# Rope partners by transfers and two packed products in the first attention of a four-layer transformer kernel

## What is computed

```python
xn = layernorm(x)                                  # over the 128 features
q, k, v = (xn @ W + b, split into 2 heads of 64)   # for Wq, Wk, Wv
# features 0..31 of a head are "content", 32..63 are "spatial"
q_spatial, k_spatial = rope(q[..., 32:]), rope(k[..., 32:])
#   rope: x1, x2 = first 16, last 16 of the spatial features
#   [x1 * cos - x2 * sin, x1 * sin + x2 * cos]
attn = softmax(q @ k.T / sqrt(64))                 # 256 x 256 for each sequence and head
x = x + (attn @ v) @ Wo + bo
```

## Time and profile before

| | |
|---|---|
| three executions, us | 712.37, 713.66, 716.26 (median 713.66) |
| the profiled execution, us | 717.27 |
| its span, us | 715.5 |
| busy share of the span: PE / weight loads / DVE / ACT / POOL | 92% / 64% / 70% / 63% / 59% |
| granted TensorE clock, mean | 0.98 of full speed |
| DMA traffic | 52.47 MB |

### The profile page before, as it was taken

One profiled execution on the slowest core, in us unless ns is written; L12 is line 12 of the kernel. 1 busy time (PEld: TensorE's weight loads), 2 busy tenths in 40 slices (PEclk: granted clock), 3 DMA queues, 4 the chain that ended last, 5 costly groups with the idle time before them and its releaser, 6 DMA issues.

```text
span 715.5 us, 14025 instructions
## 1 busy us (share of the span) xinstructions
PE 657.6 (92%) x4713; PEld 457.9 (64%) x4716; DVE 497.8 (70%) x958; ACT 450.6 (63%) x801; POOL 425.5 (59%) x443
## 2 busy tenths in 40 slices
PE   3789998689999999997999999998989999999997
PEld 1455555477777877665555555554546777787785
DVE  6769998665657768556788888885678566775521
ACT  3668887446566666545676677775765556566664
POOL 4544543267777786633345645653666777778673
PEclk9989999899999999999999999998999999999999
DMA  6101230000000000560457666663221000000000
GB/s 195 41 22 42 53 42 2 1 1 1 1 0 0 0 1 2 162 245 7 149 186 235 210 211 225 231 205 137 77 80 47 1 15 16 15 0 15 16 16 29
DMA packets 33028, 52.47 MB, mean 73 GB/s; under 512 B 4560, under 2 KB 9680, under 8 KB 32976
## 3 DMA queue, kind: packets, MB, share of 16 engines
q1 hardware_dynamic: 32784, 51.53, 23.0%
q10 hardware_dynamic: 192, 0.26, 0.1%
HBM read 27.15 MB, written 24.38 MB: 72 GB/s over the span
## 4 chain that ended last, share of the span: by engine, by line
PE 63%; DVE 14%; ACT 8%; issue 7%; DMA 4%; POOL 1%; SPq 1%; DVEq 0%; ACTq 0%; POOLq 0%
PE banks L220 60%; ACT b_prob L1525 4%; DVE xn L182 2%; DVE a_mx L652 2%; ACT a_prob L553 2%; DMA f_h_lo<-b_k_dram 2%; DMA b_o_dram<-b_o 1%; PE banks L212 1%; DVE f_gate L1088 1%; DMA b_k_dram<-b_k_lo 1%; DVE f_h_hi L1091 1%; PE banks L977 1%; DVE f_hidden L1094 1%; DVE a_prob L666 1%; ACT f_g_hi L1044 1%
## 5 line engine op out<-in xcount | busy, mean ns | idle before, releaser
L1158 POOL TENSOR_TENSOR f_g_lo<-f_gelu,f_g_hi 128x512 fp32r<-128x512 f32 x127 | 162.9, 1291 | 54.0 <-ACT f_g_hi L1044 53.4
L1043 ACT ACTIVATE f_gelu<-banks,cols 128x512 f32<-128x512 f32 x128 | 88.3, 690 | 130.6 <-PE banks L220 108.6
L1624 DVE TENSOR_REDUCE b_segment_max<-banks 128x6 f32<-128x768 f32 x128 | 120.2, 950 | 31.1 <-PE banks L220 30.4
L1741 POOL TENSOR_SCALAR_AFFINE_SELECT b_prob<-b_prob 128x512 f32<-128x512 f32 x128 | 81.6, 638 | 93.5 <-ACT b_prob L1525 92.8
L220 PE MATMUL banks<-f_g_hi,whi 128*128 128x512 f32 x320 | 130.2, 407 | 1.9 <-POOL f_g_lo L1158 1.4
L220 PE MATMUL banks<-f_g_lo,whi 128*128 128x512 f32 x320 | 126.7, 396 | 0.0
L1525 ACT ACTIVATE b_prob<-banks 128x768 f32<-128x768 f32 x128 | 102.4, 807 | 38.5 <-PE banks L220 38.2
L1151 POOL TENSOR_TENSOR f_h_lo<-f_hidden,f_h_hi 128x512 fp32r<-128x512 f32 x60 | 77.5, 1292 | 64.5 <-DVE f_hidden L1094 62.8
L220 PE MATMUL banks<-f_h_hi,whi 128*128 128x512 f32 x256 | 104.5, 408 | 5.4 <-POOL f_h_lo L1151 2.7
L220 PE MATMUL banks<-f_h_lo,whi 128*128 128x512 f32 x256 | 101.7, 397 | 0.0
L1044 ACT ACTIVATE f_g_hi<-banks,cols 128x512 fp32r<-128x512 f32 x128 | 87.4, 683 | 0.0
(11 more groups left out here) (125 smaller groups left out, 1093.6 us busy)
## 6 DMA issues: line engine op xcount, KB each, us to landing
f_h_hi<-b_q_dram SPq DMA_DIRECT2D x16, 512.0 KB, 4.0
f_h_lo<-b_k_dram SPq DMA_DIRECT2D x16, 512.0 KB, 5.0
b_o_dram<-b_o SPq DMA_DIRECT2D x8, 1024.0 KB, 4.4
b_q_dram<-b_q_hi SPq DMA_DIRECT2D x16, 256.0 KB, 3.2
b_k_dram<-b_k_hi SPq DMA_DIRECT2D x16, 256.0 KB, 3.0
w_stage<-in_wF SPq DMA_DIRECT2D x8, 352.0 KB, 3.3
b_q_dram<-b_q_lo SPq DMA_DIRECT2D x8, 256.0 KB, 3.6
b_k_dram<-b_k_lo SPq DMA_DIRECT2D x8, 256.0 KB, 3.2
```

Source lines behind the costliest of these rows:

```text
L1043: nc.scalar.activation(gf[c % 2][:, :], z_bank[c % 2], ACT.Gelu, scale=scale).then_inc(s_gf, 1)
L1158: nc.gpsimd.tensor_tensor(lo[:, c, :], gf[c % 2][:, :], hi[:, c, :].bitcast(F32), ALU.subtract).then_inc(s_glo[c % 2], 1)
L1624: nc.vector.reduce_max(seg[:, g, s, 2 * p:2 * p + 2, :], first_pass[:, 2 * p:2 * p + 2, 0:3 * P].rearrange("p b (c k) -> p b c k", c=3), A ...
L1741: nc.gpsimd.affine_select(out=pr, in_=pr, compare_op=ALU.is_ge, fill=0.0, base=0, pattern=[[0, 4], [1, P]], channel_multiplier=-1).then_in ...
```

## The change

- The columns of Wq and Wk are reordered on the host into two matrices of 128 columns: "content" (the 32 content features of q and k of both heads) and "spatial" (the same of the spatial ones). Two products take the place of four. The factor 1/sqrt(64) moves into the q rows.
- ScalarE copies the spatial product out of its bank and adds the bias (`act_raw`). Eight transfers of 16 rows swap the halves of each group of 32 rows (`sp_moves`), VectorE multiplies the copy by the cosines (`dve_spatial`) and the swapped copy by the sines (`dve_swapped`), GpSimd adds them, once a block.
- ScalarE copies the content product (`act_content`). Four transfers of 32 rows bring its parts to `qT` and `kT`, and four more bring the spatial parts. The scores wait for all eight.
- The probabilities are not scaled. The output product is made for each head apart, and VectorE adds it to x with the inverse sum as the factor, tile by tile (`dve_update`, 8 instructions a block).
- The maximum is negated in the reduction. The shift is made on GpSimd. The statistics are taken a block sooner (`b.after(3)`).
- The pieces of weights are issued between the transfers of the blocks.

```diff
@@ sp_program, sp_moves (new)
                 sp.dma_start(X[:, 2 * TILES:, :], x_dram[:, 2 * TILES:, :]).then_inc(s_x2, 16)
+                blocks = [Block(i // 2, i % 2) for i in range(BLOCKS)]
+                for n in blocks:
+                    sp_moves(sp, n)
+                    if n.t >= 1:
+                        for piece in blocks[2:4] if n.t == 1 else blocks[n.t + 2:n.t + 3]:
+                            ffn["sp_piece"](sp, piece, False)
+            PIECES = HA * 2
+            ROWS_A = P // PIECES
+            SWAPS = 2 * PIECES
+            def sp_moves(sp, n):
+                t = n.t
+                half = ROWS_A // 2
+                wait(sp, s_tu, t)
+                sp.wait_ge(s_raw, t + 1)
+                for at in range(0, P, ROWS_A):
+                    for to, of in ((at, at + half), (at + half, at)):
+                        sp.dma_start(swapped[to:to + half, :], raw[of:of + half, :]).then_inc(s_sw, 16)
+                wait(sp, s_sc, SEQS * (t - 1))
+                sp.wait_ge(s_co, t + 1)
+                for g in range(PIECES):
+                    h, to = g // 2, (qT, kT)[g % 2][n.odd]
+                    sp.dma_start(to[DA * h:DA * h + HALF_A, :],
+                                 content[ROWS_A * g:ROWS_A * (g + 1), :]).then_inc(s_mc, 16)
+                sp.wait_ge(s_ro, t + 1)
...
@@ products
+            def pe_T(pe, n):
+                wait(pe, s_vr, n.t)
+                norm.pe(pe, n, misc)
+            def pe_spatial(pe, n):
+                pe.wait_ge(s_xT, n.t + 1)
+                wait(pe, s_raw, n.t)
+                project(spatial_bank, wA[:, W_SPATIAL, :], xnT[n.odd][:, :]).then_inc(s_ws, 1)
...
@@ pe_body
                 pe_scores(pe, b, 1)
                 if one:
-                    pe_proj(pe, n1, "k")
-                for h in (1, 0):
+                    if before:
+                        pe.wait_ge(s_done, b.t - 1)
+                    pe_v(pe, n1)
+                for h in range(HA):
                     pe_probT(pe, b, 0, h)
-                if one:
-                    pe_proj(pe, n1, "kr")
+                if two:
+                    pe_T(pe, n2)
                 pe_pv(pe, b, 0)
-                if one:
-                    pe_proj(pe, n1, "v")
+                if two:
+                    pe_spatial(pe, n2)
...
                     pe_out(pe, b.after(-1))
                 if one:
                     pe_scores(pe, n1, 0)
...
@@ act_body
-                act_normalise(act, b, 0)
                 if before:
                     act_out(act, b.after(-1))
-                for h in (1, 0):
+                if two:
+                    norm.act_apply(act, n2)
+                for h in range(HA):
                     act_probT(act, b, 0, h)
+                if two:
+                    act_xT(act, n2)
                 act_exp(act, b, 1)
                 if two:
-                    norm.act_apply(act, n2)
-                act_normalise(act, b, 1)
-                if two:
-                    act_xT(act, n2)
+                    act_raw(act, n2)
+                    if not is_block(b, 0):
+                        ffn["beside"]["act"](act, n2)
...
                     act_exp(act, n1, 0)
+                if two:
+                    act_content(act, n2)
@@ dve_swapped, dve_update, dve_body
+            def dve_swapped(dve, n):
+                dve.wait_ge(s_sw, 16 * SWAPS * (n.t + 1))
+                wait(dve, s_ro, n.t)
+                nc.vector.tensor_tensor(as_seqs(turned[:, :]), as_seqs(swapped[:, :]),
+                                        S[:, :].unsqueeze(1).to_broadcast([P, SEQS, T]), ALU.mult).then_inc(s_tu, 1)
...
+                for s in range(TILES):
+                    x = X[:, bass.ds(TILES * b.t + s, 1), :]
+                    last = nc.vector.scalar_tensor_tensor(
+                        out=x, in0=tiles_of(bank)[:, s:s + 1, :], scalar=inv[b.odd][:, s // 2, h, s % 2:s % 2 + 1],
+                        in1=x, op0=ALU.mult, op1=ALU.add)
...
                 dve_max(dve, b, 1)
...
+                    dve_v(dve, n1)
+                if three(b):
+                    dve.wait_ge(norm.shift, b.t + 1)
+                    norm.dve_stats(dve, b.after(3))
...
+                    dve_inverse(dve, b.after(-1))
+                    dve_update(dve, b.after(-1), 0, content_bank)
                 if one:
                     dve_max(dve, n1, 0)
...
+                    dve_update(dve, b.after(-1), 1, misc)
+                if two:
+                    dve_spatial(dve, n2)
+                    dve_swapped(dve, n2)
                     ffn["beside"]["dve"](dve, n2)
```

More of the change, by code:

```diff
@@ L339, in attention_a @@
             s_in_ = sem("a_inverse_total")
-            s_no = [sem(f"a_probabilities_normalised{h}") for h in range(HA)]
             s_pt = [sem(f"a_probabilities_transposed{h}") for h in range(HA)]
@@ L531, in pe_last @@
                 nxt["pe_gate"](pe, FIRST_BLOCK, 1, parts)
-                for h in (0, 1):
+                for h in range(HA):
                     pe_probT(pe, LAST_BLOCK, 1, h)
@@ L663, in dve_normalise @@
[L663 to L673 removed]
+                wait(dve, s_ex, UNITS * (b.t - 1) + HA * (s + 1))
@@ L675, in dve_body, with three @@
+            def three(b):
+                return not (isinstance(b.t, int) and b.t > BLOCKS - 4)
             def dve_body(dve, b, before, one, two):
```

324 lines of the change are left out of this document (147 added, 177 removed).

## The result

| | before | changed |
|---|---|---|
| median, us | 713.63 (4 runs, 712.37 to 716.26) | 734.59 (4 runs, 731.32 to 736.71) |
| ratio, 95% interval | | 1.0285 (1.0235 to 1.0335) |
| profiled execution / its span, us | 717.27 / 715.5 | 731.32 / 729.3 |
| granted TensorE clock, mean | 0.98 | 0.973 |
| TensorE busy share | 92% | 88% |

The changed kernel is 21 us slower (2.9%).

A forecast was written before the change was run, and what follows sets the result against it. VectorE, 93% busy in steady blocks, was taken to bound the kernel. Start +8.4, blocks 0 and 1 +2.4, five blocks -4.4 and end +0.5 sum to +6.9 us: median 720.6 us, range 713.0 to 729.5.

The forecast's parts named there:

- the issue interval: On SP, between two transfers issued in a row: 0.45 us, with 0.34 and 0.6 kept for the range.
- Rival 2: Swap issues on SP as slow as stores, 0.6 us and 2.3 to landing: +17, or 730.7 us; chance 0.16 with Rival 3.
- the ring: Steady blocks: sine product through v, transpose, exponentials and new copy to the next swaps; 7.3 us, 12.45 with the swaps.
- Start, +8.4: Before block 0's sequence 1 scores: two rounds of swaps delay the first maximum, scores at 33.4 for 25.01 us.
- Blocks 0 and 1, +2.4: First two blocks, counted from the scores, with TensorE at the lower clock: 33.5 us against 31.1.
- Five blocks, -4.4: Blocks after 0 and 1: one of 12.0 us and four of 12.45, 61.8 us for 66.2.
- End, +0.5: Block 7's output added to x within the feed-forward layer, by 8 matmuls and 8 updates: 0 to 1.5 us more on VectorE.
- any change of over 1 us in the layers behind: Sign that the forecast is wrong: layers after the changed attention, which the change does not touch, shift by over 1 us.
- The rows brought to `qT` and `kT` have room: After the swaps land these moves take 5.5 us, and the scores come after about 7.
- The floor: TensorE's work a block, the least pace: 12.6 - 1.2 + 0.5 = 11.9 us.
- The far form of rival 1: Quick, hidden transfers, TensorE at full clock in blocks 0 and 1, pace 11.4 us: -5, or 708.5 us; chance 0.10.
- Rival 3: VectorE's sine product shut out by GpSimd's add, 1.27 us a block, 7 times: 729.5 us; chance 0.16 with Rival 2.

The follow-up runs named there:

- the kernel with two queues: The changed kernel with its 16 transfers, four of a block's eight swaps issued by ScalarE and four by SP: 725.13 us (one run).
- the three quickest versions: Changed kernel with six transfers a block, 713.05 us; also with the start reordered on VectorE, 709.93; also with weight-piece counts behind the statistics, 708.89.

## Why the prediction was wrong

**The step that failed is the issue interval.** "I take 0.45, as the plain two-dimensional pieces are nearest, and keep 0.34 and 0.6 for the range." Measured: 0.63 us from issue to issue, above even the upper end. The nearest rows were not the pieces but the stores of the earlier trace rows, each 0.61 to 0.63 long and 0.67 apart: a pair of pieces in 0.92 us is one interval alone, and the case here is eight in a row. The landing, 2.0 us, was right (1.9). Two of the prediction's own signs of being wrong showed it: an interval of 0.6 us and a pace over 13.2. Rival 2, "issues as slow as the stores", was the case that came, with 730.7 for 734.59; its start (+11.7) was nearly as measured (11.5), its five blocks (+1 for 5.2) were not.

The interval is not all. At the first feed-forward matmul the kernel is 19.3 us behind, 12.4 us more than the sum of +6.9: some 7 us are the interval (start, blocks 0 and 1, four blocks of the ring), 2 us the first of the five blocks, which was taken to be bound by TensorE, and 4.4 us the last two blocks, where most is a lower clock that the prediction put at nothing; the end gives 0.7 us back.

By the terms of the sum:
- **Start, +8.4: measured +11.5.** 18 intervals lie on it; 18 x 0.18 = 3.2 us more. The mechanism, with VectorE idle for the second swaps, was right, and the order that makes it so was confirmed by undoing it (4.0 us).
- **Blocks 0 and 1, +2.4: measured +2.9.** As forecast, with a mean granted clock of 0.68 from 25 to 50 us (0.86 before), and TensorE waiting 7.15 us for v in block 1. The longer interval alone should have added 7 x 0.18 = 1.3 us here, so the fit is partly luck. Keeping the clock up won 2 us in block 0.
- **Five blocks, -4.4: measured +5.2,** a miss of 9.6 us in three parts. The ring was right in its members: 7.3 plus 7 x 0.63 plus 1.9 gives 13.6, measured 13.4 to 13.5, where 12.45 had been forecast, so some 3.2 us over the four blocks. The first block, put at TensorE's floor of 12.0, took 13.96: the ring held it too, and 2 us are there. The last two took 14.94 and 16.35, some 4.4 us over the ring. In each the clock fell behind a wait of 2 us for v, which accounts for 1.6 and 1.8 us; the rest stands beside the standstill of 1.96 us ahead of the last scores. The prediction charged the lower clock to the start alone. A pace set by a wait of 2 us a block, in place of a full TensorE, brings that risk into each block.
- **End, +0.5: measured -0.2** (from scores (7,1) to the first feed-forward matmul 7.46 us for 7.70), just under its bounds of 0 to 1.5. The updates that stand behind that matmul are not in this number. The sign "any change of over 1 us in the layers behind" did show (580.0 us for 585.5), but the traces of all kernels differ there by as much.
- **"The rows brought to `qT` and `kT` have room"** held for the change by a small margin only. Without the swaps they are what bounds the pace (12.0), and with four more issues they bind at 15 to 17 us. The prediction costed the leg behind the swaps, but not the ring that starts at the content copy: it should have stood beside the first.
- **The floor,** 11.9 to 12.0, was measured 11.6 with six transfers. The far form of rival 1 asked for a pace of 11.4 and quick transfers; the same compute with six issues in place of 16 shows it was no idle case.
- **Rival 3** did not occur in the change: all sine products of the steady part took 0.69 us, and GpSimd was idle when each began. It did occur in the kernel with two queues, in five of six blocks. The Trainium skill's rule ("SBUF — State Buffer", "SBUF: two separate sides"), by which such a VectorE operation and a GpSimd one exclude each other for a whole instruction, was seen at work there: 2.15 us for 0.68.

What stays open: whether a wait of 2 to 3 us lowers the clock differed between blocks and runs (2.76 us went without in one kernel and cost 2.9 us in another), and the runs of the three quickest versions spread over 11 to 14 us. Their profiles, one each, do not tell how much of that is the clock and how much the wait behind the branch.

## To carry to other kernels

Count the issues of a queue that stand in each ring, at 0.6 us each whatever their size (32 to 128 KB here), add some 2 us of landing (1.9 to 2.6 here), and do so for every ring that passes through the queue, not only for the one that binds today. Then lay out the data so that few transfers do: rows interleaved on the host made two transfers of eight, and six of sixteen, at nearly the same cost each, and turned a loss of 2.9% into a tie (0.998), and into about 1% less time than before (0.990) once the start and the counts were put in order. Put behind the critical instruction what it does not need: a product of the next block and a count of weights, both waiting for something late, cost 4 and 3 us.

## What was new about the hardware

- An issue on SP takes 0.59 us and follows the last by 0.63, for 16, 32 and 64 rows of 2 KB and also for 16 rows of 512 bytes (six in 3.76 us). Landing is 1.9 us at 32 KB, 2.0 at 64 KB and 2.0 to 2.6 at 128 KB (medians). A row step of 2 costs no issue time, and swaps of 64 rows landed no later with it (2.0) than without (2.6).
- Four issues on ScalarE's queue hold ScalarE for 3.0 us.
- Two waits of TensorE of equal length (1.97 and 1.99 us) can end at the full and near the lower clock.
- Behind a conditional branch TensorE stood for 1.6 to 2.8 us in most programs, and for 9.7 and 11.3 us in both profiles of the one that had 23 products more ahead of it.
